# Two attention stages of a 12-block decoder: output products earlier in TensorE's row, and VectorE's sums of one half between the first passes of the next row

## What is computed

```
qh = (q @ Wq).reshape(B, N, NUM_HEADS, HEAD_DIM)
kh, vh = (kv @ Wk).reshape(...), (kv @ Wv).reshape(...)
attn = softmax(einsum('bhnd,bhmd->bhnm', qh, kh) * HEAD_DIM ** -0.5)
out = einsum('bhnm,bhmd->bhnd', attn, vh) ... @ Wo + bo
x = _layernorm(x + out)
```

```
qf, kf = taylor_exp(q), taylor_exp(k)      # 1, x, x^2 features
mask = jnp.tril(jnp.ones((CHUNK, CHUNK)))
```

## Time and profile before

| | |
|---|---|
| time, median of 3 runs (lowest, highest) | 3875.63 us (3863.5, 3886.42) |
| the profiled execution: time, span | 3882.2 us, 3880.4 us |
| busy share over the span: PE, PEld, DVE, ACT, POOL | 78%, 59%, 58%, 38%, 32% |
| granted clock of TensorE, mean | 0.885 |
| softmax stage, from the release of the stage before to its own last norm | 1907.4 to 2315.4 us |
| Taylor stage, likewise up to its last addition | 2640.5 to 3015.8 us |

### The profile page before, as it was taken

The page is one execution under the profiler, slowest core; times in us unless marked ns, Lnnn a source line. Parts: engine busy times, 40 slices in busy tenths (PEclk is TensorE's granted clock), DMA queues, the critical chain, the costliest instruction groups (busy, mean ns, idle before and its releaser), DMA issues.

```text
span 3880.4 us, 88421 instructions
## 1 busy us (share of the span) xinstructions
PE 3013.2 (78%) x33512; PEld 2300.5 (59%) x33512; DVE 2256.3 (58%) x6293; ACT 1475.3 (38%) x2818; POOL 1253.4 (32%) x1353
## 2 busy tenths in 40 slices
PE   6886998689977986887688875966999759566592
PEld 5665776467754764665566654744767448444372
DVE  3565776668855454454477775445676454465544
ACT  2332443344432432343355542534666215202141
POOL 3553222100013353222133337143333043510445
PEclk9998998999988997999899986987999659886696
DMA  6000000000000230000100002220000113200132
GB/s 236 3 3 9 2 2 13 7 6 6 4 32 22 88 81 18 3 3 24 53 9 9 9 16 63 70 59 10 2 2 1 41 33 94 73 7 31 41 107 73
DMA packets 135416, 132.47 MB, mean 34 GB/s; under 512 B 25728, under 2 KB 113792, under 8 KB 134016
## 3 DMA queue, kind: packets, MB, share of 16 engines
q1 hardware_dynamic: 118656, 93.60, 7.6%
q0 software_dynamic: 16384, 33.59, 2.9%
HBM read 69.44 MB, written 57.67 MB: 33 GB/s over the span
## 4 chain that ended last, share of the span: by engine, by line
PE 62%; DVE 17%; ACT 9%; issue 7%; POOL 3%; DMA 1%; DVEq 0%; SPq 0%; POOLq 0%; ACTq 0%
PE banks L664 7%; ACT arena L1454 6%; DVE arena L1477 4%; PE banks L1258 4%; PE banks L1271 4%; PE banks L685 4%; PE banks L1228 3%; PE banks L1276 3%; PE banks L1738 3%; PE banks L2672 3%; PE banks L1709 3%; PE banks L1677 2%; PE banks L1700 2%; PE banks L674 2%; PE banks L1671 2%
## 5 line engine op out<-in xcount | busy, mean ns | idle before, releaser
L1477 DVE TENSOR_REDUCE arena<-banks 128x16 f32<-128x2048 f32 x128 | 289.5, 2262 | 305.3 <-PE banks L1258 305.3
L1115 POOL DMA_INDIRECT arena<-yd,arena x256 | 246.6, 963 | 321.2 <-DMA yd<-arena 247.2
L1957 POOL TENSOR_TENSOR arena<-arena 128x1024 f32<-128x1024 f32 x128 | 242.6, 1901 | 283.9 <-DVE arena L1923 283.9
L664 PE MATMUL banks<-weights,arena 128*128 x1120 | 328.2, 411 | 0.2
L1454 ACT ACTIVATE arena<-banks 128x1024 f32<-128x1024 f32 x256 | 248.2, 1021 | 182.8 <-PE banks L1276 182.8
L1487 DVE RECIPROCAL arena<-banks 128x256 f32<-128x256 f32 x128 | 223.4, 1748 | 130.9 <-PE banks L1317 70.2
L2192 POOL TENSOR_TENSOR t_var_eps<-t_meanvar,eps 128x4 f32<-128x4 f32 (+1 forms) x144 | 28.4, 197 | 818.0 <-DVE t_meanvar L2183 817.7
L774 ACT ACTIVATE arena<-banks 128x256 f32<-128x256 f32 (+2 forms) x320 | 124.0, 387 | 360.4 <-PE banks L664 357.8
L2069 POOL TENSOR_TENSOR var_eps<-meanvar,eps 128x4 f32<-128x4 f32 (+1 forms) x80 | 15.8, 197 | 703.6 <-DVE meanvar L2047 683.5
L984 DVE TENSOR_TENSOR arena<-arena,banks 128x176 f32<-128x176 f32 (+2 forms) x240 | 102.2, 426 | 223.4 <-ACT arena L774 219.1
L685 PE MATMUL banks<-weights,arena 128*128 (+2 forms) x1440 | 217.5, 279 | 2.4 <-ACT arena L786 1.7
(11 more groups left out here) (280 smaller groups left out, 7335.3 us busy)
## 6 DMA issues: line engine op xcount, KB each, us to landing
arena<-xd SPq DMA_DIRECT2D x320, 64.0 KB
yd<-arena SPq DMA_DIRECT2D x160, 128.0 KB
xd<-zeros SPq DMA_DIRECT2D x4, 4352.0 KB, 28.3
weights<-in_w_L_ffn SPq DMA_DIRECT2D x1, 4372.5 KB, 13.7
arena<-yd,arena POOLq DMA_INDIRECT x256, 2.5
weights<-in_w_L_ffn SPq DMA_DIRECT2D x1, 3076.0 KB, 11.3
xd<-x_state,arena POOLq DMA_INDIRECT x192, 2.2
weights<-in_w_L_ffn SPq DMA_DIRECT2D x1, 2980.5 KB, 10.3
```

Source lines behind the costliest of these rows:

```text
L664: ins = eng.matmul(dst, b.xt[:, k % 2, :], w[:, bass.ds(at + n * inner, inner)], start=True, stop=True)
L1115: eng.indirect_dma_start(b.g[:, at % G_RING, k, :], None, yd[0:(i // GROUPS + 1) * HALF * P, :], bass.IndirectOffsetOnAxis(b.slot_y[:, n:n ...
L1477: eng.tensor_reduce(b.max[:, n % 2, :].rearrange("p (g s) -> p g s", g=4)[:, :, 0:4], b.s[:, :, :, :], AX_X, ALU.max).then_inc(sem["s_max" ...
L1957: eng.tensor_tensor(probs, probs, bcast(b.rec[:, n % 2, hs], 2, P), ALU.mult)\
```

## The change

1. In TensorE's odd iterations the two output products move forward: `output(out, 0)` straight behind the scores, `output(out, 1)` between the first two groups of transposes.
2. In the Taylor stage's odd iterations v2 and v3 move backward: from ahead of the first two groups of transposes to ahead of the last two. ScalarE's copies follow the same order.
3. VectorE alternates: the sums of half 0, the next row's first pass of half 0, the sums of half 1, the next row's first pass of half 1 (before: both sums, then both first passes).
4. The tail addition comes behind both first passes in the softmax stage, and between the sums of half 1 and the first pass of half 1 in the Taylor stage. The norm of the group before (`dve_tail_norm`) moves to the end of the even iteration.
5. Two instruction forms change on VectorE: the epsilon is added with a `tensor_tensor` and a small constant tile, and the norm of these two stages is a `scalar_tensor_tensor` with a broadcast column, where both were `tensor_scalar`.

```diff
@@ pe_lines
                 if n + 1 < batch:
                     scores(n + 1)
-                if items:
+                if e == 0 and items:
                     project(*items[0])
+                if out is not None:
+                    output(out, 0)
                 if row:
                     transposes(n - 1, 0)
-                if e and items:
-                    project(*items[1])
+                if out is not None:
+                    output(out, 1)
                 if row:
                     transposes(n - 1, 1)
-                if out is not None:
-                    output(out, 0)
                 if e == 0 and items:
                     project(*items[1])
                 if row:
                     values(n - 1, 0)
+                if e and items:
+                    project(*items[0])
+                if row:
                     transposes(n - 1, 2)
-                    if len(items) == 4:
-                        project(*items[2])
+                if len(items) == 4:
+                    project(*items[2])
+                elif e and items:
+                    project(*items[1])
+                if row:
                     transposes(n - 1, 3)
-                elif len(items) == 4:
-                    project(*items[2])
-                if out is not None:
-                    output(out, 1)
                 if len(items) == 4:
                     project(*items[3])
...
@@ dve_lines
-                    eng.tensor_scalar(b.den[:, hs], b.sum[:, hs], 2e-12, None, ALU.add).then_inc(sem["p_eps"], 1)
+                    eng.tensor_tensor(b.den[:, hs], b.sum[:, hs], const("tiny")[:, 0:8], ALU.add)\
+                       .then_inc(sem["p_eps"], 1)
...
+            def added(i):
+                eng.wait_ge(sem["o_ps"], after["o_ps"](0, i + 1))
+                dve_tail_add(eng, l, i, psum[7][:, 0:2 * P].rearrange("p (e c) -> p e c", e=2))
...
                 if n < batch:
                     sums(n, 0)
-                    sums(n, 1)
-                if e == 0 and n >= 4:
-                    dve_tail_norm(eng, l, i - 2)
                 if n + 1 < batch:
                     first_pass(n + 1, 0)
-                if e and n >= 3:
-                    eng.wait_ge(sem["o_ps"], after["o_ps"](0, i))
-                    dve_tail_add(eng, l, i - 1, psum[7][:, 0:2 * P].rearrange("p (e c) -> p e c", e=2))
+                if n < batch:
+                    sums(n, 1)
+                if e and n >= 3 and p["taylor"]:
+                    added(i - 1)
                 if n + 1 < batch:
                     first_pass(n + 1, 1)
                 if e and n >= 3:
+                    if not p["taylor"]:
+                        added(i - 1)
                     dve_tail_stats(eng, l, i - 1)
+                if e == 0 and n >= 4:
+                    dve_tail_norm(eng, l, i - 2)
...
@@ dve_tail_norm
+                if p["kind"] == "lines":
+                    ins = eng.scalar_tensor_tensor(
+                        out=dst, in0=tail_source(l, i, r, t), scalar=t_meanvar[:, t, 0:1],
+                        in1=t_rstd[:, t:t + 1].to_broadcast([P, P]), op0=ALU.subtract, op1=ALU.mult)
```

More of the change, by code:

```diff
@@ L206 @@
 SOURCE = {"L0_self": "a", "L0_mlp1": "xo", "L0_cross": "a", "L0_mlp2": "xo", "L1_mlp": "xo"}
-CONSTS = [("ident", P), ("take", 4 * P), ("halves", 2), ("ones", 32), ("eighths", P), ("slots", 4), ("first", P), ("lower", P), ("heads16", 16), ("heads8", 8), ("heads4", 4), ("heads2", 2),
+CONSTS = [("ident", P), ("take", 4 * P), ("halves", 2), ("tiny", 8), ("ones", 32), ("eighths", P), ("slots", 4), ("first", P), ("lower", P), ("heads16", 16), ("heads8", 8), ("heads4", 4), ("heads2", 2),
           ("diagonal", P), ("iota", 8),
@@ L1863, in act_lines @@
                     transposed(n - 1, 0)
-                if e and items:
-                    projected(*items[1])
-                if row:
                     transposed(n - 1, 1)
@@ L1873, in act_lines @@
                     values_out(n - 1, 0)
+                if e and items:
+                    projected(*items[0])
+                if row:
                     transposed(n - 1, 2)
@@ L1876, in act_lines @@
                     projected(*items[2])
+                elif e and items:
+                    projected(*items[1])
                 if row:
@@ L2209, in dve_tail_norm @@
                 dst = res[:, t, :] if in_place else state["x"][:, i * g + t, :]
-                ins = eng.tensor_scalar(dst, tail_source(l, i, r, t), t_meanvar[:, t, 0:1],
-                                        t_rstd[:, t:t + 1], ALU.subtract, ALU.mult)
+                if p["kind"] == "lines":
+                    ins = eng.scalar_tensor_tensor(
+                        out=dst, in0=tail_source(l, i, r, t), scalar=t_meanvar[:, t, 0:1],
+                        in1=t_rstd[:, t:t + 1].to_broadcast([P, P]), op0=ALU.subtract, op1=ALU.mult)
+                else:
+                    ins = eng.tensor_scalar(dst, tail_source(l, i, r, t), t_meanvar[:, t, 0:1],
+                                            t_rstd[:, t:t + 1], ALU.subtract, ALU.mult)
             ins.then_inc(sem["tail_step"], 1)
@@ L3213, in const_arrays @@
     f = {"ident": row == col, "ones": np.ones((P, 32)), "first": (row == 0) & (col >= 0),
-         "eighths": (col % 32 < 8) & (row >= 0), "slots": row % 32 // 8 == np.arange(4), "halves": row % 32 // 16 == np.arange(2),
+         "eighths": (col % 32 < 8) & (row >= 0), "slots": row % 32 // 8 == np.arange(4), "halves": row % 32 // 16 == np.arange(2), "tiny": np.full((P, 8), 2e-12),
          "take": -1.0 * np.concatenate([(row % 32 == s) & (col >= 0) for s in range(4)], 1), "lower": col <= row, "heads16": row // 8 == np.arange(16),
```

## The result

The changed kernel takes 3927.14 us (median of 4 runs, 3915.57 to 3940.33), the kernel before 3875.03 us on the same chips (4 runs): a ratio of 1.0138, 95% interval 1.0103 to 1.0174, slower by 52 us. The forecast was 3934 us, +58.

A forecast was written before the change was run, and what follows sets the result against it. TensorE was taken to bound both stages, busy 85% (softmax) and 90% (Taylor). Softmax -26 and Taylor +84 gave +58 us, on a median of 3875.6 us a forecast of 3934 us, range 3900 to 3962.

The forecast's parts named there:

- Softmax, the wait: Softmax stage: the scores' wait of 2.36 us for the first pass's subtraction goes, all 14 times, -33.5 us.
- Softmax, the clock: Softmax stage: the half clock behind those waits goes too, 12 x 1.5 us, -18 us.
- Softmax, the gaps: Odd softmax rows: two uncovered gaps between transposes and `values`, 1.7 us a row in 15 rows, +25.5 us.
- The sum of -26 us: Softmax stage: the wait, clock and gap terms together, -33.5 - 18 + 25.5.
- Taylor, the stall: Odd Taylor rows: v2 waits for the tail addition, TensorE idle 3.0 us; row +4.3 us, 14 rows, +60 us.
- Taylor, the clock: Odd Taylor rows: half clock behind the idle time, v2 to second `values` +1.6 us, 14 times, +22.5 us.
- Taylor, the last row (n = 31): Taylor stage, n = 31: no first pass queued, addition follows the output at once, row 13.38 us, +1.3 us.
- Costs at nothing: Instruction forms, norm's move, exchange of sums and first pass, and constant tile: no cost, VectorE having over 100 us spare.
- my bound of 1.24 us: VectorE: upper bound for the two new instruction forms, from the same operation on 1024 elements a partition.
- No stall at v2: Rival, Taylor stage: VectorE reaches the addition once the output is done; only gaps, +19 - 26 = -7, 3869 us; chance 0.10.
- -51 without the gaps: Softmax stage: the wait's -33.5 us and the clock's -18 us, before the uncovered gaps' +25.5 us.

The follow-up runs named there:

- e3: Kernel before with one move: in the softmax stage VectorE does the tail addition behind both first passes; 3844.8 us, ratio 0.99.
- e4: Kernel before with VectorE's changed order in the softmax stage only and the new instruction forms in both stages; 3826.88 us, ratio 0.9868.
- e5: Changed kernel with the tail addition of odd Taylor rows moved behind the sums of half 0, ahead of the next first pass; 3869.27 us, ratio 0.9989.
- e6: Changed kernel with TensorE kept busy in the odd Taylor rows' stall by repeating the second group of transposes five times; 3913.06 us, ratio 1.0113.
- e7: Changed kernel with the two new instruction forms undone (tensor_scalar again for epsilon and norm); 3924.65 us, ratio 1.0122.
- e10: e3 with the norm moved to the end of the even row, old form, sums and first passes not alternated; ratio 0.9896 against the kernel before.
- e9: e3 with the norm as scalar_tensor_tensor in both stages, in its old place behind the two sums; ratio 0.99 against the kernel before.
- e2: Kernel before with the changed order in the Taylor stage only, new instruction forms in both stages; 3948.23 us, ratio 1.0223.

## Why the prediction was right, step by step

- **Softmax, the wait.** Right: 14 waits of 2.36 us are gone, and e3 shows that it was the addition's place, not the outputs'.
- **Softmax, the clock.** Right: no slow scores are left from row 2 on, and the granted clock is 1.00 there.
- **Softmax, the gaps.** Right: 1.7 us forecast for an odd row, 11.24 - 9.62 = 1.62 measured against e4. The sum of -26 us is what the stage shows (408.0 to 382.0).
- **Taylor, the stall.** Right, and e5 isolates it: v2 at 10.63 us of the row, forecast 10.9; 3.03 us idle, forecast 3.0; 14 rows.
- **Taylor, the clock.** The mechanism was right, the size too large: the term of +1.6 us a row is 1.28 (e6). I priced it from a stretch in which v2 ran at half clock (2.08 us) and the last transposes at full clock again (0.60); here, in 13 of 14 rows, the clock falls only about 1 us after TensorE has resumed, so v2 escapes it and v3 and the last transposes don't. That, and the stall's 0.3 us a row, is why the Taylor stage grew by 77 and not 84 us. The Trainium skill's rule that the prediction cites, a loop that starts every burst at half rate and pays in every turn ("TensorE: Matmul & The Clock Gate", section "HAM oscillation — how this bites in real kernels"), held for the paying in all 14 rows; a start at half rate shows only in the first.
- **Taylor, the last row (n = 31).** Wrong in the step, small in size. No first pass is queued there, but both sums still stand ahead of the addition, so v2 waits 1.41 us; from the last scores to the end of the stage it is 33.8 us against 31.4, +2.4 and not +1.3.
- **Costs at nothing.** Right for the forms in the changed kernel (e7), though my bound of 1.24 us for them was not: beside GpSimd's multiplication the norm in the new form takes up to 1.98 us. For the norm's place I put nothing; it was worth 10.5 us with the outputs where they were (e3 to e10). What it is worth with the changed TensorE order no run shows.
- **The rivals.** "No stall at v2" gave 3869 us for the case that VectorE reaches the addition in time. e5 makes just that case, and took 3869.27. That the two agree to the decimal is luck: I had +19 us for the Taylor stage, it grew by 14 (378.2 to 391.9), and the totals scatter by more than the difference.

What I did not see at the time is that the good part needs none of the moves on TensorE. My own figures said so: -51 without the gaps, -26 with them.

## What to carry to other kernels

When a product is moved earlier in an engine's order, look up what it used to cover, and which instruction of the consumer frees its buffer: here bank 7 was freed by an addition that stood behind work which itself waited for something queued behind the moved product. Moving only the consumer that waits too early (the addition, and the norm that ran beside GpSimd) made the softmax stage 51 us shorter (408.0 to 357.1), with TensorE's order untouched; the total fell by 47 us, on two runs. A stage's length and its rows' starts, which here repeat within some 0.1 us where TensorE's clock holds, tell effects of 10 us apart that the totals do not: single runs of the kernel before lie between 3849.5 and 3896.2 us.

## What the runs showed of the hardware

A slowed GpSimd was new to me. In the Taylor stage of the changed kernel its multiplication (three figures: shortest, median, longest ns) is slow in 16 of 64 cases; alone it takes 1.9 us:

```profile
L1968 POOL TENSOR_TENSOR arena<-arena x64: 1895/1897/2978, 2639.6 to 3060.6; 128x1024 f32<-128x1024 f32 x64
```

The slow ones start together with VectorE's `masked`, which now can fall beside them:

```profile
2725.07 1.21 DVE L1918 TENSOR_REDUCE arena<-arena 128x8 f32<-128x1024 f32 x1
...
2726.79 1.23 DVE L1911 SCALAR_TENSOR_TENSOR arena<-arena,consts 128x1024 f32<-128x1024 f32 x1
2726.79 2.98 POOL L1968 TENSOR_TENSOR arena<-arena 128x1024 f32<-128x1024 f32 x1 [4.25 <-DVE arena L1928]
```

In all 16 a `masked` starts within 0.2 us of it. 2.98 us is 1.9 plus most of the 1.23 of `masked`. In the softmax stage the first pass reads one input from PSUM and one from SBUF, and no multiplication there is longer than 1900 ns. The Trainium skill ("SBUF — State Buffer", section "Who interferes with whom") says that GpSimd and a VectorE instruction with two SBUF inputs, or one in a two-port mode, exclude each other from a shared pair of ports for the whole instruction. The traces agree, in both directions: GpSimd waits here, and in e9 the norm, rewritten with two SBUF inputs, waits for GpSimd (1428 ns on average) as it does in the form of before (two instructions of 0.81 and 1.93 us in e3, the second ending with GpSimd's). In which mode the old form ran, no trace here shows.

The clock need not fall at once: with TensorE idle from 2707.8 us on, the granted clock was still 1.00 at 2711, 0.50 from 2712 on and 1.00 again by 2716, so that the work which pays isn't the work that waited. In the softmax stage of before it fell within 0.3 us of the scores' start at 2093.09. Nor does it fall each time: behind a wait of 2.36 us it fell 12 times of 14 in the kernel before and 10 of 14 in e2, behind 3.03 us 14 times of 14 in the changed kernel and in e2.
